# The low part of the experts' turned rows: from a TensorE product to ScalarE and GpSimd

## The chip, the cores and the metric

One core of one Trainium2 chip. The time is the device time of one execution in microseconds; three runs of the kernel before gave 1327.05, 1329.67 and 1331.39 us, median 1329.67.

## What is computed

A block of a gated cross-attention transformer, on 2048 rows of 512 elements in fp32:

```python
x = x + tanh(g_xattn[0]) * xattn(_layernorm(x), ctx, ...)
x = x + tanh(g_ffn[0]) * ffn(_layernorm(x), ...)

# ffn: xt is [2048, 512], 16 experts of inner size 352, 4 of them per row
scores = softmax(xt @ Wg.T)
...
h = silu(einsum('td,eid->eti', xt, W1)) * einsum('td,eid->eti', xt, W3)
expert_out = einsum('eti,edi->etd', h, W2)
y = einsum('etd,te->td', expert_out, combine)
z = silu(xt @ Ws1.T) * (xt @ Ws3.T) @ Ws2.T
return (y + z)
```

The change is in the part with the experts.

## The kernel before

The kernel runs in stages, one after the other: projections and attention (to about 600 us), the closing of attention, the shared expert and the routing (to about 757 us), and then the experts, `stage_experts` (L1446 to L1689), to the end at 1330 us. In the experts' stage the rows that the routing gave to each expert are packed into tiles of 128 rows, 79 tiles in all, and each tile belongs to one expert. An expert of five tiles fills 640 places.

Accuracy is kept by splitting. Every operand of a matmul is written as a high part in fp32r, a shorter form of fp32, and a low part, which is what is left, also in fp32r. A product then has three passes (`PASSES`, L1619): high by high, high rows by low weights, low rows by high weights. Only the third pass needs the rows' low part.

What the engines do for one tile g, in the order in which their queues hold it:

- GpSimd gathers the tile's rows from DRAM four tiles ahead (L101, an indirect DMA, called at L1556).
- TensorE turns the rows, four transposes of 128x128 into the PSUM tile `e_xps` (`turn_x`, L1621). ScalarE copies `e_xps` to the high part `xT[:, 0]` (L1568). TensorE then adds minus the high part to `e_xps`, by one product with minus the unit matrix, `k_lessr` (`take_high`, L1630), so that `e_xps` holds the low part, and ScalarE copies it to `xT[:, 1]` (L1570). The transposes open the sum in PSUM (start at the first, stop at none) and `take_high` closes it.
- TensorE makes the gate and the up product, twelve matmuls each (`first`, L1636). ScalarE takes silu of the gate (L1589) and copies up (L1593), GpSimd multiplies the two to `h` (L1551).
- TensorE turns `h` (`turn_h`, L1646). ScalarE copies the result twice, as high part and as plain fp32 `e_hc` (L1574, L1575), and GpSimd subtracts one from the other to get the low part (`low_h`, L1538).
- TensorE makes the down product, nine matmuls (`down`, L1652), ScalarE scales it to `e_y` (L1582), and GpSimd adds the rows to the output by an indirect DMA (`scatter`, L1535). Each scatter waits until the one before has landed (L1532).

The tiles are staggered by hand. In TensorE's `body(g)` the order is: look up which weight buffer holds the tile's expert (`look_up`, L1609, which also waits for the weights' low part), gate of g, turn h of g-1, up of g, turn x of g+1, down of g-1; the product of `take_high` for g+1 lies in the down product of g-1, ahead of its third pass (L1658). GpSimd's order per tile is: low part of h of g-1, product h of g, scatter of g-2, gather of g+4. ScalarE's is: silu of g, two copies of h of g-1, copy of up of g, the copies of x of g+1, result of g-1.

The experts' weights have two buffers. SyncE loads the weights of an expert when the up and the down product of the last tile of the expert two before it are done (L1496 to L1500). VectorE splits what has landed in nine cuts, a cast (L1511) and a subtraction (L1518) each, for the 15 experts from the second on.

Semaphores start at 1 (`begin`), so a wait for g + 2 is a wait for the tile g itself.

Of the kernel before, what the change touches and what calls it, by code (L numbers as in the profile page):

```python
# [9 lines left out]
F32 = mybir.dt.float32  # L10
# [6 lines left out]
P = 128  # L17
BATCH, SEQ, D = 4, 512, 512
T = BATCH * SEQ
KD = D // P  # L20
# [1425 lines left out]
def stage_experts(nc, io, dram, out):  # L1446


    with ExitStack() as c:
# [9 lines left out]
        hT = [sb(f"e_hT{i}", [P, 2, NI, P], F32R) for i in range(2)]  # L1459
        y = [sb(f"e_y{i}", [P, D]) for i in range(XB)]  # L1460

        upc, hc = sb("e_upc", [P, INTER]), sb("e_hc", [P, NI, P])
        xps, hps, yps = ps("e_xps", [P, KD, P]), ps("e_hps", [P, NI, P]), ps("e_yps", [P, D])
        gate = [ps(f"e_gate{i}", [P, INTER]) for i in range(2)]
        up = [ps(f"e_up{i}", [P, INTER]) for i in range(2)]
        s_pad, s_xsub, s_x = sem("e_spad"), sem("e_sxsub"), io["s_rows"]
        s_w, s_out = io["s_w"], [dsem(f"e_sout{i}") for i in range(XB)]
        s_upc, s_xt, s_xT, s_xlow, s_gate, s_up, s_act, s_h, s_ht, s_hT, s_hlow, s_down, s_y, s_high, s_low = (
            sem(f"e_s{n}") for n in ("upc", "xt", "xT", "xlow", "gate", "up", "act", "h", "ht", "hT", "hlow", "down", "y",
# [54 lines left out]

        @block.gpsimd
        def _(eng):
            begin(eng, s_pad, s_h, s_hlow)
            def scatter(g):
                n, last = g % XB, (g - 1) % XB
                eng.wait_ge(s_y, g + 2)  # L1530
                if g:
                    eng.wait_ge(s_out[last], 16 * ((g - 1) // XB + 1))  # L1532
                else:
                    eng.wait_ge(io["s_base"], 16 * NT)
                eng.indirect_dma_start(out=out, out_offset=bass.IndirectOffsetOnAxis(ap=io["scatter"][:, g:g + 1], axis=0),  # L1535
                                       in_=y[n][:], in_offset=None, compute_op=ALU.add).then_inc(s_out[n], 16)

            def low_h(g, r):  # L1538
                eng.wait_ge(s_hT, 2 * g + 3)
                eng.tensor_tensor(hT[r][:, 1], hc[:], hT[r][:, 0].bitcast(F32), ALU.subtract).then_inc(s_hlow, 1)  # L1540

            for r in range(2):
                eng.memset(h[r][:, INTER:], 0.0).then_inc(s_pad, 1)  # L1543
            eng.wait_ge(s_pad, 3)
            for g in range(TILES):
                r = g % 2
                if g:
                    low_h(g - 1, 1 - r)
                eng.wait_ge(s_upc, g + 2)
                eng.wait_ge(s_act, g + 2)  # L1550
                eng.tensor_tensor(h[r][:, 0:INTER], act[r][:], upc[:], ALU.mult).then_inc(s_h, 1)  # L1551
                if g >= 2:
                    scatter(g - 2)
                if g + XB < TILES:
                    eng.wait_ge(s_xt, g + 2)
                    gather_rows(eng, io, dram, g + XB)  # L1556
            low_h(LAST, LAST % 2)
            scatter(LAST - 1)
            scatter(LAST)
            for n in range(XB):  # L1560
                eng.wait_ge(s_out[n], 16 * ((TILES + XB - 1 - n) // XB))

        @block.scalar
        def _(eng):
            begin(eng, s_upc, s_xT, s_xlow, s_act, s_hT, s_y)
            def part_x(g, r):
                eng.wait_ge(s_xt, g + 2)
                eng.activation(xT[r][:, 0], xps[:], ACT.Copy).then_inc(s_xT, 1)  # L1568
                eng.wait_ge(s_xsub, g + 2)
                eng.activation(xT[r][:, 1], xps[:], ACT.Copy).then_inc(s_xlow, 1)  # L1570

            def part_h(g, r):
                eng.wait_ge(s_ht, g + 2)
                eng.activation(hT[r][:, 0], hps[:], ACT.Copy).then_inc(s_hT, 1)  # L1574
                eng.activation(hc[:], hps[:], ACT.Copy).then_inc(s_hT, 1)  # L1575

            def result(g, n, u):

                eng.wait_ge(s_down, g + 2)
                if not isinstance(u, int) or u:  # L1580
                    eng.wait_ge(s_out[n], 16 * u)
                eng.activation(y[n][:], yps[:], ACT.Copy, scale=io["scale"][:, bass.ds(g, 1)]).then_inc(s_y, 1)  # L1582

            def body(g, n, u):
                r = n % 2
                eng.wait_ge(s_gate, g + 2)
                if not isinstance(g, int) or g >= 2:
                    eng.wait_ge(s_h, g)
                eng.activation(act[r][:], gate[r][:], ACT.Silu).then_inc(s_act, 1)  # L1589
# [12 lines left out]
            result(LAST, LAST % XB, LAST // XB)  # L1602

        @block.tensor
        def _(eng):
            begin(eng, s_xt, s_xsub, s_gate, s_up, s_ht, s_down)
            word, due, now, before = (eng.alloc_register(n) for n in ("word", "due6", "now", "before"))

            def look_up(g):  # L1609

                eng.reg_load(word, io["ready"][0:1, bass.ds(g, 1)])
                eng.reg_mov(before, now)
                eng.reg_alu(now, word, 1, ALU.bitwise_and)
                eng.reg_alu(due, word, 1, ALU.logical_shift_right)
                buffers = [eng.snap(reg, min_val=0, max_val=1) for reg in (now, before)]
                eng.wait_ge(s_low, eng.snap(due, min_val=1, max_val=(CUTS + 1) * E + 1))
                return buffers
# [3 lines left out]
            def turn_x(g, n, u):  # L1621
                eng.wait_ge(s_x[n], 16 * (u + 1))
                if not isinstance(g, int) or g:
                    eng.wait_ge(s_xlow, g + 1)
                for k in range(KD):
                    mm = eng.matmul(xps[:, k, :], x[n][:, k * P:(k + 1) * P], io["ident"], is_transpose=True, start=k == 0, stop=False,  # L1626
                                    skip_group_check=True)
                mm.then_inc(s_xt, 1)

            def take_high(g, r):  # L1630

                eng.wait_ge(s_xT, g + 2)
                eng.matmul(xps[:].rearrange("p k n -> p (k n)"), io["lessr"], xT[r][:, 0].rearrange("p k n -> p (k n)"), start=False, stop=True,  # L1633
                           skip_group_check=True).then_inc(s_xsub, 1)

            def first(g, r, buf, col, out, done):  # L1636
                for mine, its in PASSES:
                    if mine:
                        eng.wait_ge(s_xlow, g + 2)
# [9 lines left out]
                    mm = eng.transpose(hps[:, n, :], h[r][:, n * P:(n + 1) * P], io["ident"])  # L1649
                mm.then_inc(s_ht, 1)  # L1650

            def down(g, r, buf, turned=None):  # L1652
                eng.wait_ge(s_hT, 2 * g + 2)
                if not isinstance(g, int) or g:
                    eng.wait_ge(s_y, g + 1)
                for mine, its in PASSES:
                    if mine:
                        if turned is not None:  # L1658
                            take_high(turned, r)
                        eng.wait_ge(s_hlow, g + 2)  # L1660
                    for n, (_, size) in enumerate(ICH):
                        at = W13 + n * D
# [4 lines left out]
            def body(g, n, u):  # L1667
# [8 lines left out]
                if exists(g + 1):  # L1676
                    turn_x(g + 1, (n + 1) % XB, u + (n + 1) // XB)
                if exists(g - 1):
                    down(g - 1, 1 - r, last, g + 1 if exists(g + 1) else None)
                elif exists(g + 1):  # L1680
                    take_high(g + 1, 1 - r)

            eng.wait_ge(s_pad, 3)
            turn_x(0, 0, 0)
            take_high(0, 0)
            eng.reg_mov(now, 0)
            tiles(eng, body)
            turn_h(LAST, LAST % 2)
# [79 lines left out]
```

## Time and profile before

| What | Value |
|---|---|
| median of three runs | 1329.67 us |
| profiled execution | span 1330.1 us, first to last instruction (the page gives no time of its own beside it) |
| experts' stage | 757 to 1330 us |
| busy in the whole span | TensorE 1261.9 us (95%), VectorE 659.6 (50%), ScalarE 587.1 (44%), GpSimd 639.0 (48%) |
| mean granted TensorE clock | 0.981 |

A profile is one execution. Times in a timeline are microseconds from the first instruction. Matmuls are pipelined: the record of one is longer than the step from its start to the next one's start, and it is the step that counts. GpSimd's rows of an indirect DMA are the time in which it writes descriptors, the landing is the transfer. "Issue" is waiting for nothing that the profile shows. PEld is TensorE's loading of weights, which runs beside the matmuls.

### The profile page before, as it was taken

What the parts mean: (1) busy time and instruction counts of PE and PEld (TensorE: products, weight loads), DVE (VectorE), ACT (ScalarE), POOL (GpSimd) and SP (SyncE); (2) the same over time, 40 slices, a digit from 0 to 9 for tenths busy, and PEclk for the clock granted to TensorE, in tenths of its full rate; (3) what the DMA queues carried; (4) which work ended last, traced back from release to release, by engine and by line L of the source; (5) the groups of instructions that cost most, each with busy time, mean ns of one, the idle gap of its engine ahead of it and who ended that gap; (6) DMA issues with size and microseconds to landing.
All of it is one profiled execution on the core that took longest, in us unless ns stands there. A gap on an engine that the chain in (4) does not pass through costs nothing. (4 is left out here: it accounts for less than half of the span.)

```text
span 1330.1 us, 27215 instructions
## 1 busy us (share of the span) xinstructions
PE 1261.9 (95%) x8457; PEld 923.6 (69%) x8458; DVE 659.6 (50%) x1862; ACT 587.1 (44%) x1018; POOL 639.0 (48%) x726
## 2 busy tenths in 40 slices
PE   7998999999997998999999899999999999999995
PEld 4554544444443345777777589999999999999994
DVE  5345788898896656766424033332353343343300
ACT  1222566666665223321223145555555455555552
POOL 6000333333333323442536256666667766767664
PEclk8998999999998999999999999999999999999998
DMA  9452333333333604000013235555666566665443
GB/s 342 153 161 94 102 109 97 111 93 105 100 108 93 193 32 190 29 36 32 32 40 121 89 73 128 143 136 139 143 144 137 137 155 174 143 158 138 78 72 40
DMA packets 73870, 152.92 MB, mean 115 GB/s; under 512 B 10725, under 2 KB 16357, under 8 KB 73049
## 3 DMA queue, kind: packets, MB, share of 16 engines
q1 hardware_dynamic: 52776, 102.37, 23.5%
q0 software_dynamic: 21040, 49.88, 18.4%
q8 instruction: 30, 0.49, 0.2%
q14 instruction: 24, 0.19, 0.0%
HBM read 97.56 MB, written 52.23 MB: 113 GB/s over the span
## 5 line engine op out<-in xcount | busy, mean ns | idle before, releaser
L208 DVE CUSTOM_DVE_ANT_0 a_mb<-a_mb,late 128x128 f32<-128x128 f32 (+3 forms) x512 | 244.5, 510 | 51.1 <-PE a_mb L189 44.5
L1511 DVE CAST e_w<-e_w 128x480 fp32r<-128x480 f32 x135 | 76.5, 567 | 304.0 <-DMA e_w<-in_w2T 299.8
L640 ACT ACTIVATE a_at<-a_eb 128x1024 f32<-128x1024 f32 (+3 forms) x256 | 179.7, 705 | 103.2 <-PE a_eb L702 102.7
L576 POOL TENSOR_SCALAR_AFFINE_SELECT a_at<-a_at 128x256 f32<-128x256 f32 x256 | 106.0, 415 | 226.1 <-ACT a_at L640 225.9
L1663 PE MATMUL e_yps<-e_w,e_hT 128*128 x711 | 197.3, 404 | 0.9 <-ACT e_hT L1574 0.9
L1642 PE MATMUL e_up<-e_w,e_xT 128*128 x948 | 171.4, 330 | 0.0
L1642 PE MATMUL e_gate<-e_w,e_xT 128*128 x948 | 169.1, 327 | 1.0 <-issue 1.0
L1642 PEld LDWEIGHTS e_gate<-e_w,e_xT 128*128 128x128 f32 x948 | 157.3, 190 | 10.5 <-issue 5.6
L1642 PEld LDWEIGHTS e_up<-e_w,e_xT 128*128 128x128 f32 x948 | 150.6, 190 | 0.0
L1663 PEld LDWEIGHTS e_yps<-e_w,e_hT 128*128 128x128 f32 x711 | 128.1, 189 | 25.5 <-issue 1.2
L189 PE MATMUL a_mb<-a_k,a_q 49*128 49x256 f32 (+2 forms) x512 | 121.1, 426 | 18.7 <-DVE a_mx L208 8.6
L1535 POOL DMA_INDIRECT out<-e_y,scatter x79 | 128.2, 1623 | 21.4 <-issue 12.7
L1540 POOL TENSOR_TENSOR e_hT<-e_hc,e_hT 128x384 fp32r<-128x384 f32 x79 | 85.8, 1086 | 109.6 <-ACT e_hc L1575 109.6
L718 PE MATMUL a_pv<-a_at,a_v 128*32 128x128 f32 (+1 forms) x2304 | 122.6, 295 | 7.7 <-POOL a_at L576 4.5
L189 PEld LDWEIGHTS a_mb<-a_k,a_q 49*128 49x128 f32 x512 | 48.0, 184 | 92.8 <-DVE a_mx L208 83.6
L702 PE MATMUL a_eb<-a_q,a_k 50*128 50x256 f32 (+2 forms) x512 | 106.0, 332 | 0.0
L1518 DVE TENSOR_TENSOR e_w<-e_w 128x480 fp32r<-128x480 f32 x135 | 100.0, 741 | 4.7
L718 PEld LDWEIGHTS a_pv<-a_at,a_v 128*32 128x32 f32 x2304 | 48.0, 108 | 74.7 <-issue 44.7
L1551 POOL TENSOR_TENSOR e_h<-e_act,e_upc 128x352 f32<-128x352 f32 x79 | 80.5, 1018 | 39.6 <-ACT e_upc L1593 38.5
L101 POOL DMA_INDIRECT e_x<-dx,gather x79 | 83.5, 1057 | 23.6 <-issue 23.5
L1378 PE MATMUL s_yps<-e_w,s_h 128*128 (+1 forms) x288 | 86.4, 429 | 0.3
L1570 ACT ACTIVATE e_xT<-e_xps 128x512 fp32r<-128x512 f32 x79 | 47.2, 597 | 81.7 <-PE e_xps L1633 81.7
(243 smaller groups left out, 1766.3 us busy)
## 6 DMA issues: line engine op xcount, KB each, us to landing
e_w<-in_w13T SPq DMA_DIRECT2D x16, 1408.0 KB, 6.2
dq<-p_parts SPq DMA_DIRECT2D x32, 256.0 KB, 2.4
a_q<-dq SPq DMA_DIRECT2D x64, 128.0 KB
do<-a_o SPq DMA_DIRECT2D x32, 256.0 KB, 2.1
e_w<-in_w2T SPq DMA_DIRECT2D x16, 512.0 KB, 5.6
a_k<-dk SPq DMA_DIRECT2D x64, 98.0 KB
e_w<-in_ctxT SPq DMA_DIRECT2D x4, 1024.0 KB, 13.8
e_w<-in_x SPq DMA_DIRECT2D x4, 1024.0 KB, 13.5
```

What stands on the lines that cost most here:

```text
L189: eng.matmul(bank(io, place(turn, j, at))[:, 0:w], io["q"][r][rows, j, ch * P:(ch + 1) * P], io["k"][r][rows, 0:w], start=True, stop=True) ...
L208: eng.tensor_tensor_reduce(out=b[:, 0:w], in0=b[:, 0:w], in1=io["late"][:, SEQ - w:SEQ], scale=1.0, scalar=3 * NEG, op0=ALU.add, op1=ALU.m ...
L576: eng.affine_select(out=square, in_=square, compare_op=ALU.is_ge, fill=0.0, base=0, pattern=[[0, 2], [1, P]], channel_multiplier=-1).then_ ...
L640: eng.activation(at[r % 2][:, ch, 2 * hp:2 * hp + 2, ch * P:SEQ], eb[hp][:, :, ch * P:SEQ], ACT.Exp, scale=0.25).then_inc(s_exp, 1)
L702: mm = eng.matmul(eb[j][:, t, n0:SEQ], k[r][rows, ch * P:(ch + 1) * P], q[r][rows, j, n0:SEQ], start=True, stop=True)
L718: mm = eng.matmul(pv[32 * h:32 * h + 32, cols], v[(r - late) % NB][:, ch, :], at[buf][:, ch, 2 * j + t, cols], start=ch == 0 and n0 == 0, ...
L1378: mm = eng.matmul(yps[i % 2][:], h[0:size, mine, n, j * P:(j + 1) * P], io["w"][0:size, bass.ds(side[1], 1), first:first + D].rearrange("p ...
L1518: eng.tensor_tensor(w[rows, r, rest], w[rows, r, rest].bitcast(F32), w[rows, r, cols].bitcast(F32), ALU.subtract).then_inc(s_low, 1)
L1535: eng.indirect_dma_start(out=out, out_offset=bass.IndirectOffsetOnAxis(ap=io["scatter"][:, g:g + 1], axis=0), in_=y[n][:], in_offset=None, ...
L1540: eng.tensor_tensor(hT[r][:, 1], hc[:], hT[r][:, 0].bitcast(F32), ALU.subtract).then_inc(s_hlow, 1)
L1642: mm = eng.matmul(out[r][:], xT[r][:, mine, k, :], w[:, bass.ds(buf, 1), its * SIDE + at:its * SIDE + at + INTER].rearrange("p b n -> p (b ...
L1663: mm = eng.matmul(yps[:], hT[r][0:size, mine, n, :], w[0:size, bass.ds(buf, 1), its * SIDE + at:its * SIDE + at + D].rearrange("p b n -> p ...
```

## The change

`take_high` and its product are gone, and with them the semaphore `s_xsub`. The transposes become plain ones that each start and stop. ScalarE copies `e_xps` twice right after each other, first to the high part and then to a new plain fp32 tile `e_xc`, of which there is one; the second copy waits until GpSimd has read the tile before. GpSimd subtracts the high part from `e_xc` and writes `xT[:, 1]`, with the place of this step in its queue between the product h of the tile g and the scatter of g-2, for the tile g+1. TensorE's transposes of the next tile wait for the second copy and not, as before, for the copy of the low part. The look-up of the weights takes at least 1 for the wait's value. The matrix `k_lessr` is still built.

```diff
-        upc, hc = sb("e_upc", [P, INTER]), sb("e_hc", [P, NI, P])
+        upc, hc, xc = sb("e_upc", [P, INTER]), sb("e_hc", [P, NI, P]), sb("e_xc", [P, KD, P])
...
         @block.gpsimd
+            def low_x(g, r):
+                eng.wait_ge(s_xc, g + 2)
+                eng.tensor_tensor(xT[r][:, 1], xc[:], xT[r][:, 0].bitcast(F32), ALU.subtract).then_inc(s_xlow, 1)
...
             eng.wait_ge(s_pad, 3)
+            low_x(0, 0)
             for g in range(TILES):
                 r = g % 2
                 if g:
...
                 eng.wait_ge(s_upc, g + 2)
                 eng.wait_ge(s_act, g + 2)
                 eng.tensor_tensor(h[r][:, 0:INTER], act[r][:], upc[:], ALU.mult).then_inc(s_h, 1)
+                if g < LAST:
+                    low_x(g + 1, 1 - r)
                 if g >= 2:
                     scatter(g - 2)
...
         @block.scalar
             def part_x(g, r):
                 eng.wait_ge(s_xt, g + 2)
                 eng.activation(xT[r][:, 0], xps[:], ACT.Copy).then_inc(s_xT, 1)
-                eng.wait_ge(s_xsub, g + 2)
-                eng.activation(xT[r][:, 1], xps[:], ACT.Copy).then_inc(s_xlow, 1)
+                if not isinstance(g, int) or g:
+                    eng.wait_ge(s_xlow, g + 1)
+                eng.activation(xc[:], xps[:], ACT.Copy).then_inc(s_xc, 1)
...
         @block.tensor
-                eng.reg_alu(due, word, 1, ALU.logical_shift_right)
+                eng.reg_alu(low, word, 1, ALU.logical_shift_right)
+                eng.reg_alu(due, low, 1, ALU.max)
...
             def turn_x(g, n, u):
                 eng.wait_ge(s_x[n], 16 * (u + 1))
                 if not isinstance(g, int) or g:
-                    eng.wait_ge(s_xlow, g + 1)
+                    eng.wait_ge(s_xc, g + 1)
                 for k in range(KD):
-                    mm = eng.matmul(xps[:, k, :], x[n][:, k * P:(k + 1) * P], io["ident"], is_transpose=True, start=k == 0, stop=False,
-                                    skip_group_check=True)
+                    mm = eng.transpose(xps[:, k, :], x[n][:, k * P:(k + 1) * P], io["ident"])
                 mm.then_inc(s_xt, 1)
 
-            def take_high(g, r):
-
+            def first(g, r, buf, col, out, done):
                 eng.wait_ge(s_xT, g + 2)
-                eng.matmul(xps[:].rearrange("p k n -> p (k n)"), io["lessr"], xT[r][:, 0].rearrange("p k n -> p (k n)"), start=False, stop=True,
-                           skip_group_check=True).then_inc(s_xsub, 1)
...
-            def down(g, r, buf, turned=None):
+            def down(g, r, buf):
...
                 for mine, its in PASSES:
                     if mine:
-                        if turned is not None:
-                            take_high(turned, r)
                         eng.wait_ge(s_hlow, g + 2)
...
                 if exists(g - 1):
-                    down(g - 1, 1 - r, last, g + 1 if exists(g + 1) else None)
-                elif exists(g + 1):
-                    take_high(g + 1, 1 - r)
+                    down(g - 1, 1 - r, last)
```

## Rows read from the trace of the kernel before

**Rows 1.** Table of windows, one of eleven alike in the experts' stage; the columns first.

```profile
core 0: us, PE busy (x) PEld busy (x) DVE busy (x) ACT busy (x) POOL busy (x), PEclk, DMA share, GB/s
900.00:950.00 50.00, 50.00 (x294) 46.21 (x293) 12.01 (x18) 25.12 (x51) 33.57 (x30) 1.00 0.61 146
```

**Rows 2.** The chain of waits between 740 and 1331 us, by line.

```profile
by line: PE e_yps L1663 27.3%; PE e_gate L1642 26.5%; PE e_up L1642 25.8%; PE e_xps L1626 5.8%; PE e_hps L1649 4.3%; PE e_xps L1633 3.2%; DMA out<-e_y,scatter 1.6%; issue 0.7%; POOL out L1535 0.3%; ACT e_xT L1568 0.2%; ACT e_upc L1593 0.2%;
```

**Rows 3.** Timeline of TensorE's matmuls: start us, us, engine line op out<-in xcount.

```profile
1046.99 0.39 PE L1633 MATMUL e_xps<-e_xT,k_lessr 128*128 128x512 f32 x1
1047.22 0.85 PE L1663 MATMUL e_yps<-e_w,e_hT 128*128 x3
1047.90 2.10 PE L1642 MATMUL e_gate<-e_w,e_xT 128*128 x12
1049.84 0.49 PE L1649 MATMUL e_hps<-ident,e_h 128*128 128x128 f32 x3
1054.84 2.10 PE L1642 MATMUL e_gate<-e_w,e_xT 128*128 x12
```

**Rows 4.** The same timeline at the first tile.

```profile
760.51 3.88 PE L1642 MATMUL e_gate<-e_w,e_xT 128*128 x12 [0.58 <-issue]
```

**Rows 5.** Groups by line, 740 to 1331 us: busy us, mean ns | idle before.

```profile
L1540 POOL TENSOR_TENSOR e_hT<-e_hc,e_hT 128x384 fp32r<-128x384 f32 x79 | 85.8, 1086 | 109.6 <-ACT e_hc L1575 109.6
L1551 POOL TENSOR_TENSOR e_h<-e_act,e_upc 128x352 f32<-128x352 f32 x79 | 80.5, 1018 | 39.6 <-ACT e_upc L1593 38.5 <-DMA out<-e_y,scatter 0.5
L101 POOL DMA_INDIRECT e_x<-dx,gather x75 | 79.3, 1057 | 22.5 <-issue 22.4
L1329 POOL TENSOR_TENSOR e_w<-s_part,e_w 128x512 f32<-128x512 f32 x3 | 3.8, 1278 | 10.5 <-ACT s_part L1287 10.5
```

**Rows 6.** Timeline of GpSimd in undisturbed tiles.

```profile
1047.01 1.60 POOL L1535 DMA_INDIRECT out<-e_y,scatter  x1 [0.19 <-issue]
1048.91 1.00 POOL L101 DMA_INDIRECT e_x<-dx,gather  x1 [0.30 <-issue]
1051.36 1.01 POOL L1540 TENSOR_TENSOR e_hT<-e_hc,e_hT 128x384 fp32r<-128x384 f32 x1 [1.45 <-ACT e_hc L1575]
1052.82 0.94 POOL L1551 TENSOR_TENSOR e_h<-e_act,e_upc 128x352 f32<-128x352 f32 x1 [0.46 <-ACT e_upc L1593]
```

**Rows 7.** Timeline of ScalarE in the tile of rows 6.

```profile
1052.28 0.47 ACT L1593 ACTIVATE e_upc<-e_up 128x352 f32<-128x352 f32 x1 [1.01 <-PE e_up L1642]
1052.72 0.60 ACT L1568 ACTIVATE e_xT<-e_xps 128x512 fp32r<-128x512 f32 x1
```

**Rows 8.** Timeline: loads of two experts, one split's first and last operation, next gate product.

```profile
941.15 0.38 SPq L67 DMA_DIRECT2D e_w<-in_w13T  x1
969.04 0.37 SPq L67 DMA_DIRECT2D e_w<-in_w13T  x1
957.40 0.41 DVE L1511 CAST e_w<-e_w 128x480 fp32r<-128x480 f32 x1 [22.47 <-DMA e_w<-in_w2T]
969.16 0.69 DVE L1518 TENSOR_TENSOR e_w<-e_w 96x512 fp32r<-96x512 f32 x1
971.34 2.10 PE L1642 MATMUL e_gate<-e_w,e_xT 128*128 x12
```

**Rows 9.** Timeline of VectorE and GpSimd where a split and a tile meet.

```profile
1142.66 1.10 DVE L1511 CAST e_w<-e_w 128x480 fp32r<-128x480 f32 x1
1142.00 1.49 POOL L1540 TENSOR_TENSOR e_hT<-e_hc,e_hT 128x384 fp32r<-128x384 f32 x1 [1.47 <-ACT e_hc L1575]
1143.47 1.09 POOL L1551 TENSOR_TENSOR e_h<-e_act,e_upc 128x352 f32<-128x352 f32 x1
1144.73 1.83 POOL L1535 DMA_INDIRECT out<-e_y,scatter  x1 [0.16 <-issue]
1146.86 1.45 POOL L101 DMA_INDIRECT e_x<-dx,gather  x1 [0.30 <-issue]
```

**Rows 10.** Timeline of a waiting scatter, and the scatters' landing times by source line.

```profile
957.36 1.67 POOL L1535 DMA_INDIRECT out<-e_y,scatter  x1 [0.99 <-DMA out<-e_y,scatter]
DMA to landing us min/median/max: 4.5/5.0/7.0
```

More of the change, by code:

```diff
@@ L1465, in stage_experts @@
         up = [ps(f"e_up{i}", [P, INTER]) for i in range(2)]
-        s_pad, s_xsub, s_x = sem("e_spad"), sem("e_sxsub"), io["s_rows"]
+        s_pad, s_xc, s_x = sem("e_spad"), sem("e_sxc"), io["s_rows"]
         s_w, s_out = io["s_w"], [dsem(f"e_sout{i}") for i in range(XB)]
@@ L1526, in _ @@
         def _(eng):
-            begin(eng, s_pad, s_h, s_hlow)
+            begin(eng, s_pad, s_h, s_hlow, s_xlow)
+            def low_x(g, r):
+                eng.wait_ge(s_xc, g + 2)
+                eng.tensor_tensor(xT[r][:, 1], xc[:], xT[r][:, 0].bitcast(F32), ALU.subtract).then_inc(s_xlow, 1)
             def scatter(g):
@@ L1564, in _ @@
         def _(eng):
-            begin(eng, s_upc, s_xT, s_xlow, s_act, s_hT, s_y)
+            begin(eng, s_upc, s_xT, s_xc, s_act, s_hT, s_y)
             def part_x(g, r):
@@ L1605, in _ @@
         def _(eng):
-            begin(eng, s_xt, s_xsub, s_gate, s_up, s_ht, s_down)
-            word, due, now, before = (eng.alloc_register(n) for n in ("word", "due6", "now", "before"))
+            begin(eng, s_xt, s_gate, s_up, s_ht, s_down)
+            word, due, low, now, before = (eng.alloc_register(n) for n in ("word", "due6", "low6", "now", "before"))
             def look_up(g):
@@ L1623, in turn_x @@
                 if not isinstance(g, int) or g:
-                    eng.wait_ge(s_xlow, g + 1)
+                    eng.wait_ge(s_xc, g + 1)
                 for k in range(KD):
-                    mm = eng.matmul(xps[:, k, :], x[n][:, k * P:(k + 1) * P], io["ident"], is_transpose=True, start=k == 0, stop=False,
-                                    skip_group_check=True)
+                    mm = eng.transpose(xps[:, k, :], x[n][:, k * P:(k + 1) * P], io["ident"])
                 mm.then_inc(s_xt, 1)
-            def take_high(g, r):
+            def first(g, r, buf, col, out, done):
                 eng.wait_ge(s_xT, g + 2)
-                eng.matmul(xps[:].rearrange("p k n -> p (k n)"), io["lessr"], xT[r][:, 0].rearrange("p k n -> p (k n)"), start=False, stop=True,
-                           skip_group_check=True).then_inc(s_xsub, 1)
-            def first(g, r, buf, col, out, done):
                 for mine, its in PASSES:
@@ L1678, in body @@
                 if exists(g - 1):
-                    down(g - 1, 1 - r, last, g + 1 if exists(g + 1) else None)
-                elif exists(g + 1):
-                    take_high(g + 1, 1 - r)
+                    down(g - 1, 1 - r, last)
             eng.wait_ge(s_pad, 3)
             turn_x(0, 0, 0)
-            take_high(0, 0)
             eng.reg_mov(now, 0)
```

## The prediction

> **What bounds the kernel now.** The change lies in the experts' stage, so I read the stage first and not the whole span. The table of windows has TensorE busy for all of each 50 us between 800 and 1300 us, at a granted clock of 1.00 (the 2.4 GHz level), while VectorE has 12 of 50 us, ScalarE 25 and GpSimd 34 [rows 1]. The chain of waits, cut to this stage, agrees: it walks over TensorE lines for nine tenths of its time and the product with minus the unit matrix, L1633, holds 3.2% of it [rows 2]. So TensorE sets the pace, everything else is hidden, and one tile takes from one gate product to the next, 1054.84 - 1047.90 = 6.94 us [rows 3], 79 times. What must be read next is how much room the engines have that take the work over, and when.
>
> **What the change removes.** One matmul and its weight load per tile. In the timeline of TensorE it starts at 1046.99 and the next product starts at 1047.22 [rows 3]: 0.23 us, though its own record is 0.39 us long, because matmuls are pipelined. The chain's 3.2% of 591 us over 79 is 0.24 us and agrees. 79 x 0.23 = **18.2 us**, all of it on the path. At the very start the first gate product stood 0.58 us behind the product and the look-up of the buffer [rows 4], and now the look-up can run while ScalarE copies: I take 0.8 us for that product and wait together, between 0 and 1.1. The next tile's gain at the start I leave at nothing, since its low part must now come from GpSimd while VectorE is already splitting weights. Sum so far **-19.0 us**; new tile time 6.71 us.
>
> **What it adds on ScalarE.** Nothing in work: the second copy of 128x512 was there before and only reads earlier. ScalarE has half its time free [rows 1]. The new wait on s_xlow stands before this copy, and behind it are the copy itself and the result copy; it asks for the subtraction of the tile before, long done. Nothing is charged, and if GpSimd ran a tile late that cover would be gone and the whole delay would land on TensorE.
>
> **What it adds on GpSimd.** A subtraction of 128x512 per tile. No row has this form with an fp32r output; the two nearest are the f32 addition of 128x512 at L1329 with 1.28 us [rows 5] and the 128x384 subtraction of L1540, whose 1.01 us undisturbed [rows 6] scales to at most 1.35. I take 1.28. It is put behind the product h of the tile and ahead of the scatter and the gather, so it delays both, and through them the next low part of h.
>
> I time one quiet tile from U, the start of the copy of up (1052.28) [rows 7]. Before: low part of h starts at U-0.92, h at U+0.54 [rows 6], the next gate product at U+2.56 [rows 3]. After: copy of xT to U+1.04 [rows 7], second copy to U+1.64, subtraction from about U+1.70 to U+2.98. TensorE's gate product starts at U+2.33, and it wants the low part for its last four of twelve matmuls: 1.94 us for twelve (1047.90 to the next group at 1049.84 [rows 3]) puts that at U+3.62, the weight load 0.2 earlier, **U+3.4**. So 0.4 us of room. The scatter then has 0.15 issue and 1.60, the gather 0.30 and 1.00 [rows 6], to U+6.03; the next low part of h could start at 6.71-0.92 = 5.79. It starts 0.24 late, ends at U'+0.33 and still leaves before h at U'+0.54. GpSimd's round is 6.3 to 6.4 of 6.71 us. In quiet tiles the cover holds, by a little.
>
> **Where it doesn't hold.** While VectorE splits an expert's weights (15 times, 12.45 us each, 957.40 to 969.85 [rows 8]) the two engines hold each other up. Spread over the 15 x 12.45 / 6.94 = 27 tiles under a split, the means of [rows 5] against the quiet 1.01 and 0.95 [rows 6] give (1.086-1.01) x 79/27 = 0.22 us for the low part of h and 0.21 for h. The subtraction, longer and coming with no gap behind another, gets 0.25 by the same rows. The gather gets 0.17 in the same way (mean 1.057), the scatter 0.1, between nothing and the 0.23 of [rows 9]. A load is issued at a U and its split starts 957.40 - 941.15 = 16.25 us later [rows 8], with the shorter tiles 16.0, that is two tiles and 2.6 us, and ends, at the 14.25 us worked out below, at U+3.4 two tiles on: two subtractions fall under each split. First: low part of h from U-0.5 to 0.73, h to 1.9, subtraction to 3.45: 0.05 to 0.1 us late. Then 3.3 us of scatter and gather bring GpSimd to U+6.8, level with the next U; low part of h to 1.25, h to 2.4, subtraction to 3.95: 0.6 us late. The third tile is quiet and has it caught up. 0.7 us x 15 = **+10.5 us**, bounds 0 (the arrivals fall well) and 27 (below).
>
> The Trainium skill, SBUF — State Buffer, section "Who interferes with whom", says that VectorE's casts and two-input operations and GpSimd's instructions take one shared pair of ports by an exclusive lock, and that the loser blocks for the whole instruction. Here a cast of 0.41 us took 1.10 beside a GpSimd operation of 1.01 us [rows 9], a delay of 0.69, less than the whole instruction; by the page each subtraction would cost the split 1.28 us and by the rows about 0.9.
>
> **What the split loses.** A split is nine pairs of a cast and a subtraction, 0.41 and 0.69 us where nothing disturbs, 9.9 us and their gaps, and takes 12.45 [rows 8]: some 2.2 us for about four GpSimd operations, 0.55 each. Two subtractions of 1.28 us more add 1.4 by that mean, 2.0 by the 0.69 us of [rows 9] scaled by length; I take 1.8. Six of the fourteen loads are 27.9 us apart (four tiles), as 941.15 and 969.04 [rows 8]. There the split ended at 969.85 and the gate product's weights were wanted at 971.34 - 0.23 = 971.11: room 1.26. After: less 5 x 0.23 = 1.15 since tiles are shorter, plus 0.7 of the stalls above, plus 0.3 as the load is let go earlier, less 1.8: 0.7 us late. What one expert is late the next has as room, so I count half for each of the six: 6 x 0.35 = **+2.1 us** (0 to 5). Experts of five tiles have over 7 us of room.
>
> **Scatters.** Each waits for the landing of the one before, 5.0 us in the median and up to 7.0 [rows 10], against a round that is now 6.71. One at 957.36 already waited 0.99 [rows 10]. It holds the gather and the next low part of h. I charge 0.1 us a load, **+1.5 us** (0 to 5). The gather itself runs four tiles ahead and is hidden by three. Building of the matrix minus one stays in the kernel, so nothing is gained at the head.
>
> Sum: -19.0 + 10.5 + 2.1 + 1.5 = **-4.9 us**. The profiled execution's span is 1330.1 us, so 1325.2; it lies 0.4 above the median 1329.67 of the three runs, so the forecast is **1324.8 us**. With the stall per split between 0.35 and 1.05 us its own range is 1319.5 to 1330.
>
> **Rivals.**
> The cover holds in the splits too: the lateness falls on VectorE, whose work has room in most experts. For it: mean delays of 0.2 us against a room of 0.4. Against: the second tile under a split starts with none. 1330.1 - 19.0 = 1311.1, as a median 1310.7.
>
> GpSimd is the bound under the splits (the other side). Its price is the worst pair of operations of [rows 9] in every such tile: low part of h 1.49, h 1.09, scatter 1.83, gather 1.45, and 1.28 + 0.48 for the subtraction. First tile: -0.5 + 1.49 + 1.09 + 1.76 = 3.84, 0.44 late; scatter and gather with issue 3.73, to 7.57, that is U'+0.42; then 4.76, 1.36 late. 1.8 us x 15 = 27 us, which hides the experts' wait: 1330.1 - 19.0 + 27 + 1.5 = 1339.6, as a median 1339.2. It decides from a stall of (19.0 - 1.5)/15 = 1.17 us a split upward. For it: back-to-back operations let VectorE in between each pair, and what GpSimd needs between a gather and the next operation was never seen tight. Against: that tile is the costliest of the 27, the mean is a third of its delay.
>
> The split becomes the bound: VectorE loses more than 0.9 us to each subtraction and the experts of four tiles wait for weights. With 1.3 us for each (the room then -1.5) and the third tile's low part disturbed as well, 6 x 0.75 = 4.5 in place of 2.1 and 0.9 in place of 0.7 a split: -19.0 + 13.5 + 4.5 + 1.5 = +0.5, about 1330.2. The lock rule of the Trainium skill's page named above would give this.
>
> Nothing happens, since the product cost nothing in place: 1329.7. The step of 0.23 us in TensorE's timeline speaks against it.
>
> **How the numbers follow.** About 0.3%, 4 us, is what can be told from no change: 1325.7 to 1333.7. Forecast 0.50 (0.29 faster, 0.20 same, 0.01 slower), cover holds 0.17 (faster), GpSimd bound 0.24 (slower), split bound 0.07 (0.04 same, 0.03 slower), nothing 0.02 (same). Faster 0.46, same 0.26, slower 0.28. The range reaches from 1313 (most of the first rival left out) to 1338 (the better half of the second in), with 2 in 10 outside.
>
> **What would show it.** L1633 gone and quiet tiles 6.71 us apart, if not, the 0.23 is wrong. GpSimd's low part of x near 1.28 us in quiet tiles and 1.5 under splits. TensorE idle before gate matmuls, released by the new GpSimd line, about 10 us in some 20 to 30 pieces, all under splits; none would mean the first rival, 20 us or more the second. Splits of 14.2 us in place of 12.45. Few us of TensorE waiting for VectorE's L1518 at an expert's first tile. It is wrong altogether if TensorE also waits in quiet tiles, or if its clock leaves 1.00 in the stage.

## The result: slower by 1.2%, because the weights' split is late

Four runs of the changed kernel gave 1339.81, 1349.10, 1349.11 and 1349.43 us, median 1349.11, against 1330.53 us for four of the kernel before. The ratio is 1.0121, 95% interval [1.0079, 1.0164]. Forecast were 1324.8 us and a range of 1313 to 1338, so both the sign and the range were wrong. The profiled execution took 1349.11 us with a span of 1347.0.

The page of the changed kernel first: busy time of the engines, then the granted clock in 40 slices.

```profile
PE 1259.6 (94%) x8378; PEld 921.5 (68%) x8379; DVE 750.8 (56%) x1862; ACT 579.2 (43%) x1018; POOL 745.8 (55%) x805
PEclk9999999999998997999999999999999898999998
```

TensorE's busy time is about what it was, although 79 matmuls are gone. VectorE has 91 us more, and none of its instructions was changed. The window over the experts' stage says the same; its columns are those of [rows 1].

```profile
755.00:1310.00 555.00, 529.87 (x3038) 488.16 (x3039) 268.76 (x271) 261.66 (x531) 462.31 (x379) 0.97 0.55 129
```

The same window of the kernel before:

```profile
755.00:1310.00 555.00, 550.00 (x3222) 508.75 (x3221) 177.31 (x271) 278.04 (x549) 367.15 (x309) 0.99 0.56 130
```

The chain of waits from 750 us to the end, by line, now goes through VectorE for a fifth of its time, where [rows 2] had none of it:

```profile
by line: PE e_gate L1645 21.0%; PE e_yps L1664 19.7%; PE e_up L1645 19.0%; DVE e_w L1518 13.7%; DVE e_w L1511 7.5%; DMA e_w<-in_w2T 4.5%; PE e_xps L1635 4.2%; PE e_hps L1652 3.4%; issue 1.6%; DMA out<-e_y,scatter 1.5%; SPq L74 0.5%; POOL ou
```

The waits of the stage, with us in total, times, and the longest:

```profile
DVE e_w L1511 <- DMA e_w<-in_w2T: 227.8, 15, 22.8
PEld e_gate L1645 <- issue: 32.6, 26, 4.6
PE e_gate L1645 <- DVE e_w L1518: 20.8, 7, 4.1
POOL e_hT L1544 <- ACT e_hc L1583: 32.2, 13, 4.9
POOL out L1539 <- DMA out<-e_y,scatter: 6.5, 3, 3.6
PEld e_yps L1664 <- POOL e_hT L1544: 0.6, 3, 0.3
PEld e_gate L1645 <- POOL e_xT L1530: 0.4, 1, 0.4
```

TensorE waits for VectorE's subtraction seven times, 20.8 us in all, up to 4.1 us each, at the first tile of an expert. For GpSimd's low parts it hardly waits: 0.6 and 0.4 us. Of the 32.6 us in which the gate's weight loads are put down to "issue", 23.8 stand before the same seven products; they are not a second loss.

**How the split gets late.** The groups of the two engines that meet, columns as in [rows 5]; the first line is VectorE's subtraction in the kernel before, both forms together, the others are of the changed kernel:

```profile
L1518 DVE TENSOR_TENSOR e_w<-e_w 128x480 fp32r<-128x480 f32 x135 | 100.0, 741 | 4.7
L1518 DVE TENSOR_TENSOR e_w<-e_w 128x480 fp32r<-128x480 f32 x120 | 164.3, 1369 | 4.2
L1511 DVE CAST e_w<-e_w 128x480 fp32r<-128x480 f32 x120 | 85.2, 710 | 231.4 <-DMA e_w<-in_w2T 227.8
L1530 POOL TENSOR_TENSOR e_xT<-e_xc,e_xT 128x512 fp32r<-128x512 f32 x79 | 108.8, 1378 | 6.0 <-ACT e_xc L1578 2.4
L1544 POOL TENSOR_TENSOR e_hT<-e_hc,e_hT 128x384 fp32r<-128x384 f32 x79 | 81.2, 1028 | 33.6 <-ACT e_hc L1583 32.2
L1556 POOL TENSOR_TENSOR e_h<-e_act,e_upc 128x352 f32<-128x352 f32 x79 | 79.1, 1002 | 18.1 <-ACT e_upc L1601 17.5
```

GpSimd's operations are nearly undisturbed: 1.03 us for the low part of h (1.09 before), 1.38 for the new subtraction. VectorE's subtraction of 128x480 went from a mean of 0.72 us to 1.37. The timelines of VectorE and GpSimd, at the end of the split ahead of the longest wait, show why:

```profile
1059.39 0.41 DVE L1511 CAST e_w<-e_w 128x480 fp32r<-128x480 f32 x1
1059.84 4.08 DVE L1518 TENSOR_TENSOR e_w<-e_w 128x480 fp32r<-128x480 f32 x1
1063.95 0.41 DVE L1511 CAST e_w<-e_w 128x480 fp32r<-128x480 f32 x1
1065.64 0.69 DVE L1518 TENSOR_TENSOR e_w<-e_w 96x512 fp32r<-96x512 f32 x1
```

```profile
1058.77 1.45 POOL L101 DMA_INDIRECT e_x<-dx,gather  x1 [0.30 <-issue]
1060.25 1.03 POOL L1544 TENSOR_TENSOR e_hT<-e_hc,e_hT 128x384 fp32r<-128x384 f32 x1
1061.22 0.95 POOL L1556 TENSOR_TENSOR e_h<-e_act,e_upc 128x352 f32<-128x352 f32 x1
1062.13 1.26 POOL L1530 TENSOR_TENSOR e_xT<-e_xc,e_xT 128x512 fp32r<-128x512 f32 x1
1063.56 1.83 POOL L1539 DMA_INDIRECT out<-e_y,scatter  x1 [0.17 <-ACT e_y L1590]
```

GpSimd's low part of h, h and low part of x follow each other without a gap, from 1060.25 to 1063.39. VectorE's subtraction of 0.66 us stands through all three and ends 0.53 us after the last: 4.08 us. In [rows 9] VectorE got in between two operations: there the copy of up that h needs had ended only at 1143.40, just before the low part of h did at 1143.49, and VectorE's cast ended 0.29 us into h's record and took 1.10. Over the stage, 21 of VectorE's 270 operations stand through three of GpSimd's and lose 3.1 us each on average, some 65 us in all; in the kernel before none lost over 0.9 us.

This split began at 1045.98, ended at 1066.33 and so took 20.35 us, the longest. All fifteen take 15.9 to 20.35 us, 18.5 on average, against 11.7 to 13.1 and 12.4 in the kernel before. TensorE's side:

```profile
1055.56 2.10 PE L1645 MATMUL e_gate<-e_w,e_xT 128*128 x12
1060.08 2.35 PE L1664 MATMUL e_yps<-e_w,e_hT 128*128 x9
1066.56 3.88 PE L1645 MATMUL e_gate<-e_w,e_xT 128*128 x12 [4.13 <-DVE e_w L1518]
1076.18 2.10 PE L1645 MATMUL e_gate<-e_w,e_xT 128*128 x12
```

```profile
1066.00:1068.00 2.00, 1.44 (x5) 1.44 (x6) 0.33 (x1) 0.00 (x0) 1.20 (x1) 0.50 0.99 206
1070.00:1072.00 2.00, 2.00 (x9) 1.93 (x8) 0.00 (x0) 1.33 (x3) 0.00 (x0) 0.50 0.02 6
1072.00:1074.00 2.00, 2.00 (x14) 1.98 (x13) 0.00 (x0) 0.17 (x1) 1.00 (x1) 0.83 0.00 0
```

TensorE stands idle for 4.13 us and then runs at a granted clock of 0.50, the 1.2 GHz level, until after 1072. Nearly 6 us at half the clock are 3 us lost. The gate product's record is 3.88 us long instead of 2.10. From one gate product to the next the timeline has 11.00 us into the late tile and 9.62 us out of it, where a quiet tile has 6.71.

Over all seven, the periods that end at a late gate product are 9.87, 11.00, 9.93, 9.96, 9.03, 10.62 and 8.91 us, which is 22.4 us above seven times 6.71; those that follow are 8.37, 9.62, 8.35, 9.61, 8.36, 8.08 and 8.27, 13.7 us above. Together 36 us. After each of the seven waits, 2.05 to 4.13 us long, the trace shows a stretch at 0.50.

### The profile page after: what moved, and what is told of

Read it like the earlier page. It is cut to its first block and busy times, and to the rows that moved or that the text cites. A ratio compares the mean times of both kernels' runs of the same rounds, so it can differ in the third digit from the quotient of the medians.

```text
span 1347.0 us, 27121 instructions
## 1 busy us (share of the span) xinstructions
PE 1259.6 (94%) x8378; PEld 921.5 (68%) x8379; DVE 750.8 (56%) x1862; ACT 579.2 (43%) x1018; POOL 745.8 (55%) x805
## 5 line engine op out<-in xcount | busy, mean ns | idle before, releaser
L1511 DVE CAST e_w<-e_w 128x480 fp32r<-128x480 f32 x135 | 94.1, 697 | 231.9 <-DMA e_w<-in_w2T 227.8
L1645 PE MATMUL e_gate<-e_w,e_xT 128*128 x948 | 178.7, 340 | 23.4 <-DVE e_w L1518 20.8
L1645 PEld LDWEIGHTS e_gate<-e_w,e_xT 128*128 128x128 f32 x948 | 164.1, 199 | 37.6 <-issue 32.6
L1664 PE MATMUL e_yps<-e_w,e_hT 128*128 x711 | 185.5, 405 | 0.9 <-ACT e_hT L1582 0.9
L1518 DVE TENSOR_TENSOR e_w<-e_w 128x480 fp32r<-128x480 f32 x135 | 174.6, 1293 | 4.7
L1530 POOL TENSOR_TENSOR e_xT<-e_xc,e_xT 128x512 fp32r<-128x512 f32 x79 | 108.8, 1378 | 6.0 <-ACT e_xc L1578 2.4
L101 POOL DMA_INDIRECT e_x<-dx,gather x79 | 88.4, 1120 | 23.6 <-issue 23.5
L1544 POOL TENSOR_TENSOR e_hT<-e_hc,e_hT 128x384 fp32r<-128x384 f32 x79 | 81.2, 1028 | 33.6 <-ACT e_hc L1583 32.2
L1590 ACT ACTIVATE e_y<-e_yps,scale 128x512 f32<-128x512 f32 x79 | 54.4, 689 | 93.6 <-PE e_yps L1664 93.6
L1597 ACT ACTIVATE e_act<-e_gate 128x352 f32<-128x352 f32 x79 | 36.8, 465 | 127.1 <-PE e_gate L1645 127.1
```

What stands on the lines that cost most here:

```text
L1511: eng.tensor_copy(w[rows, r, cols], w[rows, r, SIDE + cols.start:SIDE + cols.stop].bitcast(F32)).then_inc(s_high, 1)
L1518: eng.tensor_tensor(w[rows, r, rest], w[rows, r, rest].bitcast(F32), w[rows, r, cols].bitcast(F32), ALU.subtract).then_inc(s_low, 1)
L1530: eng.tensor_tensor(xT[r][:, 1], xc[:], xT[r][:, 0].bitcast(F32), ALU.subtract).then_inc(s_xlow, 1)
L1645: mm = eng.matmul(out[r][:], xT[r][:, mine, k, :], w[:, bass.ds(buf, 1), its * SIDE + at:its * SIDE + at + INTER].rearrange("p b n -> p (b ...
L1664: mm = eng.matmul(yps[:], hT[r][0:size, mine, n, :], w[0:size, bass.ds(buf, 1), its * SIDE + at:its * SIDE + at + D].rearrange("p b n -> p ...
```

## Experiments

Theory V: GpSimd's operations keep VectorE from its ports, that is from reading and writing SBUF, the split is late, and TensorE waits for weights. Theory G, the forecast's: GpSimd's own low parts come late. Ratios are against the kernel before. The kernel before was run again beside each group, with medians of 1332.58, 1331.16 and 1329.29 us.

**The product's worth alone.**

```diff
...
-                eng.activation(xc[:], xps[:], ACT.Copy).then_inc(s_xc, 1)
+                eng.activation(xT[r][:, 1], xps[:], ACT.Copy).then_inc(s_xlow, 1)
...
-                if g < LAST:
-                    low_x(g + 1, 1 - r)
...
```

> The changed kernel without the GpSimd subtraction: ScalarE's second copy writes the rows' low part straight away (it then holds the whole row, a part of the computation that is left out). Nothing is added to GpSimd. If the loss comes from the added GpSimd work, by whichever way, this shows the product's worth alone: 1330 - 19 = 1311 us, splits of 12.4 us as before, no wait of TensorE for VectorE. If the loss came from TensorE's own order (transposes that start and stop, the second copy's place), it stays above 1325.

1310.70 us, ratio 0.9833 [0.9795, 0.9871]. Quiet tiles are 6.71 us apart and VectorE has 183.88 us in the stage. So removing the product brings what was forecast, a little more, and all of the loss, 38.5 us between the spans 1347.0 and 1308.5, comes with the GpSimd subtraction. TensorE has one wait of 0.3 us put down to VectorE, at a tile that is not an expert's first; none had been expected.

**The load alone, on the kernel before.** GpSimd subtracts 128x512 of tiles that nobody else reads, behind h.

```diff
...
+                if g < LAST:
+                    eng.wait_ge(s_xT, g + 3)
+                    eng.wait_ge(s_extra, g)
+                    eng.tensor_tensor(jb[:], ja[:], ja[:], ALU.subtract).then_inc(s_extra, 1)
                 if g >= 2:
                     scatter(g - 2)
...
```

> The kernel before with a GpSimd subtraction of 128x512 put in between the product h and the scatter, on tiles that nobody else reads, waiting for the high copy of x. TensorE waits for none of it. Theory V (back-to-back GpSimd operations keep VectorE from its ports, the weights' split runs late and TensorE waits for weights): splits grow well over 14.3 us, TensorE waits for VectorE's L1518, and the time is above 1332, less than the changed kernel's loss of 36 us against 1311 because tiles are still 6.94 us and leave GpSimd more gaps. Theory G (GpSimd's own lateness with the low part of x is what costs): no change, 1330.

1337.57 us, ratio 1.0039 [1.0014, 1.0063]. VectorE's time in the stage goes from 177 to 226.90 us; splits take 13.9 to 18.1 us, 15.7 on average, and TensorE waits for VectorE three times, 3.7 us, and behind the first tile nowhere for GpSimd. It speaks for V: nothing on TensorE waits for this operation. The kernel also carries the changed kernel's look-up (at least 1 for the wait's value), which the kernel before with the earlier split, below, has too, with 2.4 us between medians; so the load's own part of these 5.0 us may be smaller.

**A shorter split.**

```diff
-eng.tensor_tensor(w[rows, r, rest], ...
+eng.tensor_tensor(w[rows, r, rest.start:rest.start + 64], ...
```

> The changed kernel with VectorE's subtraction of each weight cut reduced to 64 columns (the rest of the weights' low part keeps the unsplit weight: left out). A split then has some 4 us less of VectorE work. Theory V: a split ends several us earlier, TensorE's waits for VectorE vanish or nearly so, 1311 to 1320 us. Theory G: GpSimd is disturbed a little less but its chain is as long, 1335 to 1349 us.

1312.96 us, 0.9852 [0.9816, 0.9889], with no wait for VectorE, where G had 1335 or more. GpSimd's 461.86 us of the window are close to the changed kernel's 462.31, but the window holds nearly the whole stage here and not there: over the stage GpSimd has 463 us against 485, so it is relieved as well. This run speaks against G; the run that starts the split earlier, below, decides, since there GpSimd has 486 us.

**Gaps between GpSimd's operations.**

```diff
+                if g:
+                    eng.wait_ge(s_hlow, g + 1)
                 eng.wait_ge(s_act, g + 2)
                 eng.tensor_tensor(h[r][:, 0:INTER], ...
...
             def low_x(g, r):
+                if g:
+                    eng.wait_ge(s_h, g + 1)
```

> The changed kernel, nothing left out; before the product h GpSimd waits for its own low part of h to be finished, before the low part of x for its own h. Theory V, with the ports not let go between two GpSimd operations of which the second is already queued: the two gaps let one VectorE operation in each, no VectorE operation takes over 2.5 us, splits are 13 to 15 us, TensorE's wait for VectorE falls from 20.8 us to under 5, and the time is 1315 to 1328, below both kernels. Theory G: GpSimd is 0.1 to 0.3 us a tile slower still, 1350 or more. If ports are let go between operations in any case, nothing changes: 1345 to 1352.

1351.38 us, 1.0148 [1.0107, 1.0188]: a miss. The source line of VectorE's subtraction shows that the long operations went as expected, first the changed kernel (minimum, median, maximum in ns), then this one:

```profile
L1518 DVE TENSOR_TENSOR e_w<-e_w x135: 657/660/4106, 767.2 to 1259.7; 128x480 fp32r<-128x480 f32 x120, 96x512 fp32r<-96x512 f32 x15
```

```profile
L1518 DVE TENSOR_TENSOR e_w<-e_w x135: 657/1282/1993, 768.5 to 1259.1; 128x480 fp32r<-128x480 f32 x120, 96x512 fp32r<-96x512 f32 x15
```

The maximum fell from 4106 to 1993 ns, but the median doubled, and VectorE's time in the stage is still 261 us. The same blocking comes in more pieces. TensorE waits eight times, 16.9 us. So the missing gaps make the longest operation, not the sum. The clock did not fall after every wait: after 2.39, 2.40 and 2.49 us of idle TensorE went on at 1.00, while after 1.73 and 2.48 it fell to 0.50. The length of the wait alone doesn't say whether it falls.

**The same load elsewhere.** The extra subtraction of the second experiment, between the scatter and the gather.

```diff
                 if g >= 2:
                     scatter(g - 2)
+                if g < LAST:
+                    ... the four lines from above
```

> The kernel before with the same extra 128x512 subtraction on GpSimd as in the earlier run, but between the scatter and the gather instead of behind the product h. If VectorE is kept out by a chain of GpSimd operations that follow each other (low part of h, h, subtraction), an operation that stands alone costs it little: VectorE's time in the splits grows from 177 us by under 25 us, with no operation over 2 us, TensorE waits for VectorE nowhere and the time is 1330. If what counts is how long GpSimd uses the ports in all, it is as behind h: 227 us, a few waits of TensorE, 1335.

1380.37 us, 1.0365 [1.0306, 1.0424], far worse than either branch. The timelines of GpSimd and VectorE at one such place:

```profile
1069.63 1.83 POOL L1537 DMA_INDIRECT out<-e_y,scatter  x1 [0.16 <-issue]
1070.94 1.59 POOL L1560 TENSOR_TENSOR e_jb<-e_ja 128x512 fp32r<-128x512 f32 x1
1072.70 1.24 POOL L101 DMA_INDIRECT e_x<-dx,gather  x1 [0.16 <-issue]
```

```profile
1070.47 2.60 DVE L1520 TENSOR_TENSOR e_w<-e_w 128x480 fp32r<-128x480 f32 x1
```

The subtraction's record starts at 1070.94, inside the scatter's, which runs to 1071.46, and is 1.59 us long in place of 1.28. VectorE's subtraction of 0.66 us takes 2.60. VectorE's time in the stage is 273 us, and TensorE waits 29.5 us in seven pieces. The loss comes by the same path: the seven late gate products and the clock behind them make 43.6 us of the 45.0 between the spans 1375.1 and 1330.1. So a chain of three operations is not the condition. The sum of GpSimd's work isn't either: the same subtraction cost VectorE 50 us behind h and 96 us here. Why this place costs twice as much was not found.

**A write in place of a subtraction.**

```diff
-eng.tensor_tensor(xT[r][:, 1], xc[:], xT[r][:, 0].bitcast(F32), ALU.subtract)
+eng.memset(xT[r][:, 1].bitcast(F32), 0.0)
```

> The changed kernel with GpSimd's subtraction replaced by a memset of the same tile (the rows' low part is left out as zero): the same place in the chain and the same waits, but nothing is read. If VectorE is kept out by GpSimd reading two tiles, its splits shrink back towards 12.5 us each (VectorE 190 us or less in the stage) and the time is 1311 to 1316. If a write alone, or the missing gaps alone, keep it out as well, it stays at 1340 or above, less what the memset is shorter than 1.28 us.

1310.36 us, 0.9843 [0.9823, 0.9863]; VectorE 202.65 us, between the two values expected. The memset takes 0.55 us, less than half of the subtraction, so how much is owed to its reading nothing and how much to its length was not separated. These are two executions only.

**An earlier split.** The first load of an expert gets a semaphore of its own, and VectorE begins with the five cuts that lie in it.

```diff
...
-                eng.wait_ge(s_w, (e + 1) * LOAD)
+                eng.wait_ge(s_w13, e * 16)
                 for n in range(CUTS + 1):
+                    if n == W13 // SIZE:
+                        eng.wait_ge(s_w, e * 32 + 48)
```

> The changed kernel, nothing left out, with a semaphore of its own for the first load of an expert's weights (w13, 1408 KB): VectorE splits the first five of nine cuts as soon as that has landed, some 8 us before the second load. GpSimd and VectorE meet as often and as hard as in the changed kernel. If the loss is weights that come late at the experts of four tiles (theory V): TensorE waits for VectorE nowhere, its clock stays at 1.00, and the time is 1311 to 1316 us, 1% below the kernel before. If TensorE loses by GpSimd's own lateness or by anything else of the meeting: over 1335.

1320.06 us, 0.9925 [0.9903, 0.9948]. Nothing is left out, and it beats the changed kernel by 29 us and the kernel before by 0.75%. VectorE is kept as busy as ever, 263.91 us, its splits take 18.2 us on average, and TensorE never waits for it. This shows that the late weights made the loss. It is also 9.7 us by spans (1318.2 - 1308.5) above the kernel without the subtraction, and outside the 1311 to 1316 us that were expected.

> The kernel before with the same earlier split. There TensorE never waited for weights, so nothing is to be gained: 1328 to 1333 us. If it also gains, then not the change's loss is mended but something else.

The same edit on the kernel before gave 1333.57 us, 1.0024 [1.0010, 1.0038]: no gain, as expected, and 0.2% slower, just outside the 1328 to 1333 us.

**What the 9.7 us are.** In this kernel tiles of 7.0 to 7.4 us lie under the splits. One of them, TensorE and GpSimd:

```profile
1156.82 2.10 PE L1649 MATMUL e_gate<-e_w,e_xT 128*128 x12
1164.25 2.20 PE L1649 MATMUL e_gate<-e_w,e_xT 128*128 x12 [0.53 <-issue]
```

```profile
1160.08 1.46 POOL L101 DMA_INDIRECT e_x<-dx,gather  x1 [0.30 <-issue]
1161.56 1.03 POOL L1548 TENSOR_TENSOR e_hT<-e_hc,e_hT 128x384 fp32r<-128x384 f32 x1
1163.43 1.27 POOL L1534 TENSOR_TENSOR e_xT<-e_xc,e_xT 128x512 fp32r<-128x512 f32 x1
```

The gather ends at 1161.54 and the low part of h at 1162.59, 5.77 us after the start of the gate product at 1156.82; in the quiet tile of [rows 3] and [rows 6] it is 4.47 us. The next gate product follows 1.66 us after that, 0.7 us late. Two edits ask what is late. The first reads the buffer's word ahead of the down product:

```diff
...
+                if exists(g + 1):
+                    eng.reg_load(word, io["ready"][0:1, bass.ds(g + 1, 1)])
                 if exists(g - 1):
                     down(g - 1, 1 - r, last)
```

> The kernel with the earlier split, and TensorE reads the next tile's buffer word ahead of the down product instead of behind it; nothing left out. In the run with the earlier split, tiles of 7.0 to 7.4 us instead of 6.71 had the gate product 1.2 to 1.65 us behind the end of GpSimd's low part of h, though the down product itself was not held up. Theory L (the look-up stands behind the wait for the low part of h, and its time shows when GpSimd is late): the long tiles shrink, 1311 to 1316 us against 1320. Theory X (those tiles wait for the low part of x or for VectorE): no change, 1320.

1319.67 us, 0.9930 [0.9917, 0.9944]: no gain. The distance from the low part of h to the gate product fell, at the shortest, from 1.22 to 0.86 us, but the waits moved: the down product's weight load now waits for the low part of h 17 times, 5.2 us, and the gate's for the low part of x 8 times, 1.8 us. The look-up is not what costs.

> The changed kernel with only the word read ahead. The seven late experts stay, 22 us of waiting and 14 of slow clock; by theory L the 2.5 us that are left over go: 1344 to 1348 us against 1349, a difference that can hardly be told. A fall below 1335 would say that the look-up and not VectorE's late split was what TensorE waited for.

The same on the changed kernel gave 1355.50 us, 1.0207 [1.0187, 1.0228], outside what was expected. TensorE waits 26.5 us for VectorE instead of 20.8. Why an earlier read makes the split later was not found.

The second has GpSimd make the low part of x ahead of h:

```diff
+                if g < LAST:
+                    low_x(g + 1, 1 - r)
                 eng.wait_ge(s_upc, g + 2)
                 eng.wait_ge(s_act, g + 2)
                 eng.tensor_tensor(h[r][:, 0:INTER], ...
-                if g < LAST:
-                    low_x(g + 1, 1 - r)
```

> The kernel with the earlier split, nothing left out, and GpSimd makes the low part of x ahead of the product h. The low part of x starts at the same time in quiet tiles and sooner under a split; h is later, with over 1 us of room before it is turned; GpSimd's round grows by the gap before the low part of x, to 6.7 of 6.71 us. If the low part of x is what comes late in the long tiles (theory X): 1312 to 1317 us. If the low part of h is what comes late (theory L), the fuller round makes it worse: 1322 to 1335.

1341.47 us, 1.0096 [1.0077, 1.0115], worse than both theories had it. The waits of TensorE, columns as above:

```profile
PEld e_gate L1649 <- issue: 32.7, 58, 1.1
PEld e_yps L1668 <- POOL e_hT L1548: 9.1, 17, 0.9
PEld e_hps L1656 <- POOL e_h L1562: 1.3, 5, 0.4
PEld e_gate L1649 <- POOL e_xT L1534: 0.4, 1, 0.4
```

The down product waits for the low part of h 9.1 us, the gate for the low part of x 0.4 us. But the new order also makes GpSimd stand still: it waits 44.8 us for ScalarE's copy `e_xc`, in 63 tiles, and h behind it comes later too.

```profile
POOL e_xT L1534 <- ACT e_xc L1582: 44.8, 63, 5.6
```

So the low part of x does not seem to be what is late. In the kernel with the earlier split the next gate product starts 1.25 or 1.6 to 1.7 us behind the end of the low part of h in all fourteen tiles of 7.0 us or more behind the first two, which points to GpSimd's round as a whole, seen first at the low part of h; it is the likely reading, and no run shows it by itself. It would be the forecast's second term, at another operation than the one named.

## Why the prediction was wrong

**The step that failed** is "What the split loses": two subtractions cost a split 1.8 us, and six experts of four tiles lose 0.35 us each, +2.1 in all. Measured are 36 us. It priced a GpSimd operation at 0.55 to 0.69 us of VectorE's time, and rested, like the second rival, on VectorE getting in between operations that follow each other. Three things were missing in that term.

- The price for VectorE. It was scaled from the 0.55 us that an operation cost in [rows 8], where a good part of GpSimd's time fell into VectorE's favour: VectorE needs 15 x 9.9 = 149 us undisturbed and had 177, so it stood for some 28 us over 26 tiles, 1.1 us a tile, against 2.1 us of GpSimd operations. In the changed kernel it has 269 us, stands for 120 us over 39 tiles of 6.9 us, 3.1 us a tile, against 3.4 us of GpSimd operations (1.03 + 1.00 + 1.38). That is 2.0 us more a tile for a subtraction of 1.28 us. The gaps of 1.45 and 0.46 us in [rows 6], in which VectorE could slip in, are filled now; that this is the reason is not shown, since with the extra operation behind the scatter these gaps stayed and VectorE paid as much.
- The feedback. A longer split meets more subtractions. The forecast's two per split became 39/15 = 2.6.
- The clock. After the waits of 2 to 4 us TensorE ran at half speed for some microseconds; the tiles behind them lost 13.7 us in all. The forecast had no term for it and names a clock below 1.00 only as a sign that it is wrong, though its own [rows 4] show it: the first tile's gate product, behind an idle time, has a record of 3.88 us against the 2.10 of [rows 3], and the granted clock there, 760 to 766 us in the kernel before, is 0.50.

The room of an expert was worked out too small, 1.26 us less 1.15. In the kernel without the subtraction the seven splits in question end 1.0 to 2.9 us before their weights are wanted, 2.0 on average, because they begin 13.5 to 15.0 us after their load and not 16.0. A price of 1.8 us would on average have fitted into that; the 6 us by which splits grew did not. The rule that what one expert is late the next has as room only halves a lateness that had to be sized first. One more expert than the six counted ran late: the last one has no later load to be counted by, but in the kernel before its split ends at 1241.44 and its gate product starts at 1242.93, as tight as [rows 8]. A slip in the sum is small: the 0.69 us of [rows 9] scaled by length is 0.87 a subtraction, 1.75 for two and not 2.0.

**The products.** -19.0 was forecast; by spans it is 1308.5 - 1330.1 = -21.6. Tiles of 6.71 us are exact. From the first transposes to the first gate product it took 2.41 us before (758.10 to 760.51) and 1.51 after (756.75 to 758.26), 0.9 us gained where 0.8 was taken. The second tile was not left without gain, as assumed: its gate product stands 6.98 us behind the first (758.26, 765.24) where it stood 8.86 (760.51, 769.37). That is most of the rest. Of these 1.88 us, 1.21 lie ahead of the second tile's transposes (767.22 - 760.51 against 763.76 - 758.26), in the stretch at half clock that both kernels have here and that the changed one left sooner, 0.67 behind them; the forecast foresaw neither.

**GpSimd's lateness.** +10.5 was forecast. In the changed kernel it comes to 38.5 - 36 = 2.5 us; while TensorE waits for weights, GpSimd catches up. With the wait gone it is 9.7 us. That this is so near to 10.5 is in part luck, since it belongs to splits of 18.2 us that start earlier, and not to the 14.25 us of the forecast. The addition was wrong: where TensorE waits for weights, little of GpSimd's lateness shows. Nor did the operation that the step names, the subtraction under a split, hold TensorE; in the kernel with the earlier split it is more likely the low part of h. The forecast had put the delays of the meeting on GpSimd, 0.2 us an operation, while VectorE bore nearly all of them.

**Scatters.** +1.5 was forecast and nothing is seen: GpSimd waits for a landing three times, 6.5 us, against four times, 8.5 us, in the kernel before. In the kernel without the subtraction it waits 21 times, 30.6 us, and loses nothing by it.

**The rivals.** The one that came true is the third, "the split becomes the bound", with a chance of 0.07 and a price of +0.5 us in place of +17. It had the right place, the right waiting line and the lock rule beside it, but priced the subtraction at its own length, 1.3 us, where a tile under a split costs VectorE 2.0 us more, and it had no term for the clock. The second rival had the sign right with the wrong mechanism. Of what would show the forecast, the splits were to be 14.2 us long and are 18.5 on average, TensorE's idle time before gate products was to be released by GpSimd and is released by VectorE.

The Trainium skill, SBUF — State Buffer, section "Who interferes with whom", has the loser block until the first operation ends. VectorE's 4.08 us through three GpSimd operations is more than that rule, taken for one operation, gives, and VectorE's record even starts 0.41 us ahead of the first of the three. The runs show that VectorE is held; that ports are what the two share, no run shows by itself.

## What to carry to other kernels

When work is moved to an engine that shares something with another, ask first what the other engine was doing in the gaps that are filled, and what waits for that engine later; here both engines were off the path and the cost came out on a third. Cost the moved operation on the neighbour at its full length at least (here, for 1.28 us, 1.3 us a tile in the second experiment and 2.0 in the changed kernel), let the longer neighbour's work meet more of it, and compare with the room before its deadline. If the deadline is what breaks, look for an earlier start: a semaphore of its own for the first load was worth 29 us, and made the move pay by 0.75%.

## What the runs showed of the hardware

- A VectorE operation on SBUF can be held through several GpSimd operations that follow each other without a gap: 0.66 us became 4.08 (three operations), 0.41 us became 3.93 at the longest. Beside a gather or scatter alone it loses nothing: 0.00 us on average for 65 subtractions and 0.03 for 77 casts of the changed kernel.
- A GpSimd subtraction right behind a scatter of the same queue starts 0.52 us before the scatter's trace record ends, has a record of 1.59 us in place of 1.28, and holds up VectorE as well: 2.60 us for 0.66.
- A GpSimd memset of 128x512 in the same place costs VectorE 19 us in the stage (202.65 - 183.88), the subtraction 85.
- After 4.13 us of idle TensorE ran at a granted clock of 0.50 from 1066 to beyond 1072 us. Waits of 2.05 to 4.13 us were each followed by such a stretch in the changed kernel; in the run with the self-waits some of 2.4 to 2.5 us were not.
